# Expert layers' openings: one-hot tiles filled eight at a time, constants cast and row numbers multiplied in by GpSimd, and the second layer's exponentials and splits reordered

## The reference

```python
# expert layer 1, as the reference has it
logits = xf @ Wr + br
thresh = lax.top_k(logits, 2)[0][:, 1:2]
weights = softmax(where(logits >= thresh, logits, -inf))
h = gelu(einsum('td,edh->eth', xf, W1) + b1[:, None, :], approximate=False)
expert_out = einsum('eth,ehd->etd', h, W2) + b2[:, None, :]
out = einsum('etd,te->td', expert_out, weights)
```

## Time and profile before

| | |
|---|---|
| median of 3 runs | 2554.02 us (2550.81 to 2555.0) |
| the profiled execution's own time | 2552.48 us |
| its span in the trace | 2550.7 us |
| mean granted TensorE clock | 0.969 of full speed |
| PE busy | 2288.7 us, 90% of the span |
| PEld busy | 1394.3 us, 55% |
| DVE busy | 1919.7 us, 75% |
| ACT busy | 1900.7 us, 75% |
| POOL busy | 1809.4 us, 71% |
| DMA moved | 104.49 MB, mean 41 GB/s |
| opening of layer 0 in the trace | 1437 to 1483 us |
| opening of layer 1 in the trace | 2208 to 2259 us |

### The profile page before, as it was taken

One profiled execution on the slowest core, in us unless ns is written; L12 is line 12 of the kernel. 1 busy time (PEld: TensorE's weight loads), 2 busy tenths in 40 slices (PEclk: granted clock), 3 DMA queues, 4 the chain that ended last, 5 costly groups with the idle time before them and its releaser, 6 DMA issues. The chain is left out here.

```text
span 2550.7 us, 48415 instructions
## 1 busy us (share of the span) xinstructions
PE 2288.7 (90%) x16979; PEld 1394.3 (55%) x16980; DVE 1919.7 (75%) x3499; ACT 1900.7 (75%) x2979; POOL 1809.4 (71%) x1580
## 2 busy tenths in 40 slices
PE   5999999999999999999998589978988888689998
PEld 3454545444544545455544368845555555467777
DVE  7888778887778887777786556558899899676443
ACT  4787887878877878778787546638888889767555
POOL 2687877787777878787778567617787789646554
PEclk9999999999999999999999789989999999779999
DMA  5000000000000000000000365441112010375221
GB/s 151 1 1 1 27 1 1 1 1 1 27 1 1 1 1 1 1 1 1 1 1 1 107 154 144 115 102 45 46 34 50 22 43 11 105 187 140 44 42 24
DMA packets 90655, 104.49 MB, mean 41 GB/s; under 512 B 20626, under 2 KB 79971, under 8 KB 90419
## 3 DMA queue, kind: packets, MB, share of 16 engines
q1 hardware_dynamic: 68180, 78.21, 10.2%
q0 software_dynamic: 21696, 23.16, 5.7%
q10 hardware_dynamic: 544, 0.00, 0.0%
HBM read 66.65 MB, written 23.52 MB: 35 GB/s over the span
## 5 line engine op out<-in xcount | busy, mean ns | idle before, releaser
L432 POOL TENSOR_TENSOR a_acc<-a_acc,a_pf 128x512 f32<-128x512 f32 (+1 forms) x480 | 680.1, 1417 | 280.2 <-ACT a_pf L601 258.5
L906 DVE TENSOR_TENSOR a_pl<-a_pf,a_ph 128x512 f16<-128x512 f32 x448 | 470.3, 1059 | 25.1 <-ACT a_ph L607 25.1
L2221 POOL TENSOR_TENSOR c_pl<-c_pf,c_ph 128x512 f16<-128x512 f32 x320 | 377.2, 1210 | 117.1 <-ACT c_ph L2318 116.7
L601 ACT ACTIVATE a_pf<-a_psS 128x1024 f32<-128x1024 f32 (+1 forms) x288 | 281.1, 976 | 110.0 <-PE a_psS L624 102.5
L882 DVE TENSOR_REDUCE a_mx<-a_psA 128x1 f32<-128x512 f32 x504 | 330.4, 680 | 26.8 <-PE a_psA L681 25.5
L607 ACT ACTIVATE a_ph<-a_psS 128x1024 f16<-128x1024 f32 (+1 forms) x288 | 281.1, 976 | 0.0
L553 ACT ACTIVATE a_psS<-a_mb 128x1024 f32<-128x1024 f32 x255 | 248.6, 975 | 5.0
L1317 DVE TENSOR_TENSOR f_xn<-f_xn 128x256 f16<-128x256 f32 x312 | 130.0, 423 | 152.0 <-ACT f_xn L1286 106.8
L2554 DVE TENSOR_REDUCE c_wf<-c_psA 128x1 f32<-128x512 f32 x384 | 239.4, 677 | 6.2 <-PE c_psA L2390 5.3
L2311 ACT ACTIVATE c_pf<-c_psS 128x1024 f32<-128x1024 f32 x192 | 201.2, 1048 | 49.6 <-PE c_psS L2419 45.1
L776 PE MATMUL a_psO<-a_pl,a_vh 128*128 128x512 f16 (+1 forms) x544 | 206.9, 380 | 8.1 <-POOL a_pl L450 7.9
(11 more groups left out here) (366 smaller groups left out, 6311.4 us busy)
## 6 DMA issues: line engine op xcount, KB each, us to landing
f_stage<-in_L_ffn_w SPq DMA_DIRECT2D x16, 1024.0 KB
f_stage<-in_L_ffn_W SPq DMA_DIRECT2D x16, 1024.0 KB
c_kst<-c_khs SPq DMA_DIRECT2D x64, 100.1 KB, 2.2
a_cx<-in_ctx SPq DMA_DIRECT2D x4, 1536.0 KB
c_cx<-in_ctx SPq DMA_DIRECT2D x12, 512.0 KB, 4.0
f_xrow<-f_xn SPq DMA_DIRECT2D x8, 512.0 KB, 4.6
c_kst<-c_kls SPq DMA_DIRECT2D x32, 100.1 KB, 2.2
X<-in_x SPq DMA_DIRECT2D x4, 512.0 KB, 10.3
```

Of the source, the lines that this page charges most:

```text
L432: g.tensor_tensor(acc[0:k, p, :], acc[0:k, p, :], pf[0:k, q % RF, i, :], ALU.add).then_inc(s_acc, 1)
L601: act.activation(pf[0:r, q % RF, 0:k, :], psS[q % 2][0:r, 0:k, :], ACT.Exp, scale=SCALE).then_inc(s_pF, 1)
L906: v.tensor_tensor(pl[0:r, q % RP, i, :], pf[0:r, q % RF, i, :], ph[0:r, q % RP, i, :], ALU.subtract).then_inc(s_pL, 1)
L2221: g.tensor_tensor(pl[0:r, q % RP, i, :], pf[0:r, q % RF, i, :], ph[0:r, q % RP, i, :], ALU.subtract).then_inc(s_pG, 1)
```

## The change

It touches only `experts`.

- `lo` (f32) becomes `lo16` (f16) and `tid` becomes f16. The casts of `ilo`, `ihi`, `tid`, `dmp` (and `cf` in layer 1) move from DVE to GpSimd, behind its second `rstd`; GpSimd then counts s_pool up, and DVE waits for that before it fills `ohi`. In layer 1 DVE's copy of `b1` moves behind the chunk table.
- `olo` is filled by 4 instructions of eight tiles (128 x 1024) in place of 32 of one tile, and holds plain ones. The row number goes into `ohi` instead, by two multiplications on GpSimd (new semaphore s_hm), and TensorE waits for s_hm in place of s_hi.
- Layer 1: ACT's exponentials come ahead of all its splits of expert 0. DVE's split_low of expert 0 pieces 0 to 3 moves behind the lists (all eight stand there), and split_low of expert 1 pieces 0 to 3 moves behind chunk 0's turn (all eight stand there). TensorE's bias step NB2 moves behind the index products.
- The ties branch, which is taken only when a flag is above zero, reuses s_fin for s_tied.

```diff
@@ gpsimd, behind its second rstd
+            k[0] += 1
+            for to, of in ((ilo, iloi), (ihi, ihii), (tid, tidi), (dmp, dmpi)):
+                const(g.tensor_copy(to[:, :], of[:, :]))
+            if layer:
+                const(g.tensor_copy(cf[:, :], ci[:, :]))
+            g.wait_ge(s_const, k[0])
+            g.sem_inc(s_pool, 1)
@@ gpsimd, ahead of gather(0)
+            for q in range(2):
+
+                g.wait_ge(s_hi, q + 1)
+                g.tensor_tensor(ohi[:, q, :, :], ohi[:, q, :, :], tid[:, :].unsqueeze(2).broadcast_to([P, NT, HI]),
+                                ALU.mult).then_inc(s_hm, 1)
@@ scalar
             normalize(1)
-            for q in range(PH):
-                split_high(act, 0, q)
             if layer:
                 exponentials()
-            for q in range(PH, PIECES):
+            for q in range(PIECES):
                 split_high(act, 0, q)
@@ tensor
-                if layer and i == 2 * NT - 2 * NT // NLO:
-                    pe_weighted_bias(NB2)
-                pe.wait_ge(s_hi, q + 1)
+                pe.wait_ge(s_hm, q + 1)
...
-                for i in range(NB2 + 1, NT // 2):
+                for i in range(NB2, NT // 2):
                     pe_weighted_bias(i)
@@ vector
-            for to, of in ((ilo, iloi), (ihi, ihii), (tid, tidi), (dmp, dmpi)):
-                ch.step(v.tensor_copy(to[:, :], of[:, :]))
-            if layer:
-                v.wait_ge(s_b1, 1)
-                ch.step(v.tensor_copy(b1[:, :, :].rearrange("p e f -> p (e f)"), psY[1][:, 0:E * FT]))
-                ch.step(v.tensor_copy(cf[:, :], ci[:, :]))
...
-            if layer:
-                for q in range(PH):
-                    split_low(v, 0, q)
             v.wait_ge(s_rk, 1)
...
+            v.wait_ge(s_pool, 3)
             v.wait_ge(s_xst, 16 * (NQ + layer))
...
             for q in range(2):
-                for t in range(NT):
-                    ins = v.tensor_scalar(olo[:, q, t, :], ilo[:, :], lo[:, q, t:t + 1], tid[:, t:t + 1], ALU.is_equal, ALU.mult)
-                    if t % (2 * NT // NLO) == 2 * NT // NLO - 1:
-                        ins.then_inc(s_lo, 1)
+                for t in range(0, NT, 2 * NT // NLO):
+                    w = 2 * NT // NLO
+                    v.tensor_tensor(olo[:, q, t:t + w, :], ilo[:, :].unsqueeze(1).broadcast_to([P, w, P]),
+                                    lo16[:, q, t:t + w].unsqueeze(2).broadcast_to([P, w, P]), ALU.is_equal).then_inc(s_lo, 1)
...
-            for q in range(PH if layer else 0, PIECES):
+            for q in range(PIECES):
                 split_low(v, 0, q)
...
                 v.sem_inc(s_tab, 1)
-                for q in range(PH):
-                    split_low(v, 1, q)
+                v.wait_ge(s_b1, 1)
+                op(v.tensor_copy(b1[:, :, :].rearrange("p e f -> p (e f)"), psY[1][:, 0:E * FT]))
...
-                for q in range(PH, PIECES):
+                for q in range(PIECES):
                     split_low(v, 1, q)
```

More of the change, by code:

```diff
@@ L1078, in experts @@
         pos, posi = sb("pos", [P, 2, NT]), sb("posi", [P, 2, NT], I32)
-        lo, hi16 = sb("lo", [P, 2, NT]), sb("hi16", [P, 2, NT], F16)
+        lo16, hi16 = sb("lo16", [P, 2, NT], F16), sb("hi16", [P, 2, NT], F16)
         iloi, ihii, tidi, dmpi = sb("iloi", [P, P], I32), sb("ihii", [P, HI], I32), sb("tidi", [P, NT], I32), sb("dmpi", [P, IT], I32)
-        ilo, ihi, tid, dmp = sb("ilo", [P, P], F16), sb("ihi", [P, HI], F16), sb("tid", [P, NT]), sb("dmp", [P, IT])
+        ilo, ihi, tid, dmp = sb("ilo", [P, P], F16), sb("ihi", [P, HI], F16), sb("tid", [P, NT], F16), sb("dmp", [P, IT])
         void = sb("void", [P, NC, IT])
@@ L1121, in experts @@
         s_lo = sem("lo")
+        s_hm = sem("hm")
         s_id = sem("id")
@@ L1139, in experts @@
             s_fin = sem("fin")
-            s_tied = sem("tied")
         class Loop:
@@ L1396, in _ @@
                     sp.wait_ge(ties.yF, NTIE + 2)
-                    sp.dma_start(out.rearrange("b (t p) c -> p (b t) c", p=P), X[:, :, :]).then_inc(s_tied, 16)
-                    sp.wait_ge(s_tied, 16)
+                    sp.dma_start(out.rearrange("b (t p) c -> p (b t) c", p=P), X[:, :, :]).then_inc(s_fin, 16)
+                    sp.wait_ge(s_fin, 32)
         @block.gpsimd
@@ L1834, in _ @@
             op(v.tensor_scalar(posi[:, :, :], posi[:, :, :], P - 1, None, ALU.bitwise_and))
-            op(v.tensor_copy(lo[:, :, :], posi[:, :, :]))
-            op(v.tensor_tensor(hi16[:, :, :], pos[:, :, :], lo[:, :, :], ALU.subtract))
+            op(v.tensor_copy(lo16[:, :, :], posi[:, :, :]))
+            op(v.tensor_tensor(hi16[:, :, :], pos[:, :, :], lo16[:, :, :], ALU.subtract))
+            v.wait_ge(s_pool, 3)
             v.wait_ge(s_xst, 16 * (NQ + layer))
```

## The result

The change takes 2556.09 us (median of 14 runs, 2552.15 to 2562.13) against 2553.44 us for the kernel before (14 runs, 2546.89 to 2557.86). The ratio of the runs taken side by side is 1.0016, 95% interval 1.0009 to 1.0024: 4.1 us slower (0.0016 x 2553.44), between 2.3 and 6.1 us; the best value is less than the 0.2% called no difference above. The two medians by themselves are 2.7 us apart; I go by the ratio. The profiled execution took 2552.15 us (span 2550.4 us) and is the quickest of the 14, so totals of the two traces say little. I compare distances inside an opening. For layer 0 the count runs from DVE's `ohi` fills to `gidx`; for layer 1 from DVE's `rstdw` row.

The account below looks back on a forecast made before the run. DVE was taken to bound both openings up to the lists, with ACT's queue, the weights' path and chunk 2's rows behind layer 1's. Layer 0 -0.8 plus layer 1 +3.0 gave +2.2 us: 2556.2 against 2554.02, range 2549.5 to 2560.5.

Parts of the forecast that it names:

- Layer 0: Layer 0's opening up to the lists: fills save 2.6 us, contention costs 1.8 us, together -0.8 us.
- contention: GpSimd's multiplications beside DVE's fills: DVE loses 0.6 of the shared time, 1.8 us in layer 0.
- the casts: Layer 0: moving DVE's four casts (0.4 us) to GpSimd gains nothing, since DVE waits for the router's products anyway.
- rival D: New fills run at double rate: 2.1 us less in layer 0, nothing in layer 1, 2554.1 us; chance 0.05.
- E: The fills gain nothing: contention eats all 2.6 us of layer 0, 2557.0 us; chance 0.10.
- Layer 1, lists: Layer 1's opening: gidx comes 4.0 us earlier, with PE and DVE arriving together.
- The new wait of ACT: Layer 1: ACT waits 9.4 us for half 0 of expert 1, with bias copies 4 to 7 queued behind.
- Half 0 of expert 2: Layer 1, chunk 0: this weight load, requested later at 2262.6, lands 6 us after its request.
- rival B: Half 0 of expert 2 takes 9.3 us, PE restarts at its lower clock: +6.0 us, 2560 us; chance 0.22.
- the fifth piece: Layer 1, chunk 0: ACT's fifth piece of expert 2 comes 6.1 us after the first, +4.3 us against before.
- Given back: Layer 1, chunk 1: PE no longer waits for chunk 2's rows, which returns 1.3 us.
- Rival C: The gather chain sets the end, so layer 1's 4.0 us survive: -4.8 us or -6.6, put at 2548.5 us; chance 0.13.

Follow-up runs that it names:

- x4: The change with the two multiplications by the row number on DVE, between its ohi and olo fills, instead of GpSimd: 2558.14 us, ratio 1.0018.
- x2: The change with only the low splits of expert 1 pieces 0 to 3 back ahead of chunk 0's turn: 2553.44 us, ratio 1.0002.
- x5: The change without layer 1's four adding DMAs (add_base), so its output lacks the bias part: 2549.22 us, ratio 0.9977.
- x1: The change with layer 1's low splits of pieces 0 to 3 of experts 0 and 1 back in their old places: 2550.89 us, ratio 0.9992.
- x6: x1 with the two multiplications by the row number on DVE instead of GpSimd: 2549.49 us, ratio 0.9984.
- y3: x1 with layer 1's adding DMAs issued behind chunk 2's gather, once half 1 of expert 2 is in: 2552.36 us, ratio 0.9992.
- y4: The kernel before with layer 1's adding DMAs issued behind chunk 2's gather, once half 1 of expert 2 is in: 2558.13 us, ratio 1.0014.
- z3: x6 with layer 1's adding DMAs behind chunk 2's gather, without a wait for the weights: 2540.32 us, ratio 1.0016.
- z1: x1 with five small iotas on GpSimd (0.6 us) ahead of layer 1's adding DMAs: 2531.64 us, ratio 0.9988.
- x3: x1 with ACT's order and the place of bias step NB2 as in the kernel before: 2553.34 us, ratio 0.9996.
- z2: x3 with the two multiplications by the row number on DVE instead of GpSimd: 2535.60 us, ratio 1.0001.

## Why the prediction was right, and where its steps were not

The median came out 0.1 us from the forecast of 2556.2, and in the range. The kernel before measured 0.6 us lower in the larger set of runs, so the effect is +4.1 us by the ratio, not +2.2. That the median came so close is luck: the level lay 0.6 us lower than assumed and the difference of the medians (2.65 us) 0.4 us higher than forecast, and the two cancel. Step by step:

- **Layer 0, right.** Forecast -0.8, measured -1.0 (9.85 to 8.81). Fills undisturbed 4.62 us (forecast 4.5), contention 1.70 us (forecast 1.8), the casts worth nothing: `rstdw` to `ohi` is 11.85 us in both. Of the time in which a multiplication and an `olo` fill ran together (2.97 us in layer 0, 3.71 in layer 1) DVE lost 0.57 and 0.66, forecast 0.6. Rivals D and E fall: no fill ran at twice the rate (in x4 one takes 1.155 us for 128x1024), and not all of the gain was eaten. The tier table of the Trainium skill (VectorE: DVE Perf Modes), by which rival D halved the fills, isn't contradicted by that: the same page (What auto-detection actually checks) gives the doubled rate of such an operation only where every tensor is 16-bit with step ±1, and one operand of these fills is held over the inner dimension. The prediction left this condition out.
- **Layer 1, lists, right in kind.** Forecast -4.0, measured -4.65 in the change and -3.5 in x2 and x5. The difference is PE's clock in the four bias steps: a granted 0.73 of full speed on average in the profiled execution of the change, 0.50 in x2, after like idle stretches. The steps take 4.98 us at the one and 7.19 at the other. Windows of the change, then of x2 (PE, PEld, DVE, ACT, POOL busy, PEclk, DMA share, GB/s):

```profile
2229.40:2234.50 5.10, 5.02 (x19) 3.67 (x20) 5.10 (x3) 1.82 (x5) 4.16 (x2) 0.73 0.00 0
```

```profile
2230.70:2238.00 7.30, 7.23 (x19) 5.26 (x20) 7.21 (x5) 1.81 (x5) 3.86 (x2) 0.50 0.00 0
```

- **The new wait of ACT, right.** Forecast 9.4 us, measured 11.24. The request went out 24.17 us behind `rstdw` (forecast 24.7) and landed after 4.9 us (forecast 5.0). ACT came to the wait 2.4 us sooner than forecast, because of that clock; in x2, at 0.50, the wait is 10.36. That the 4.0 us of the lists would be spent by chunk 0's turn held: forecast +0.4 us, measured -0.2, and the first hidden block +0.1 (forecast +0.8).
- **Half 0 of expert 2, mis-sized: this is the step that failed.** "I take 6": it took 11.1 us, nearly twice. Its request was on time (39.94 us behind `rstdw`, forecast 40.5). I argued that it would be quicker than half 1 for its longer rows, and x5 shows how little those count: without adding DMAs half 0's packets (256 of 4 KB) pass in 3.3 us, half 1's (1024 of 1 KB) in 3.0. Half 0 lands there in 5.0 us, and what makes the rest is `add_base`: in the change its first packet goes 5.4 us behind the request (1.0 in x5), while packets of the second and third adding DMA go, and the 256 then take 5.0 us beside the fourth's. I also wrote that `add_base` starts as early as before; it starts 2.75 us earlier (34.80 against 37.55 behind `rstdw`), so the issue of the fourth adding DMA was about to end (5.36 us behind the first's start) at the request (5.14). The condition of rival B (over 8.4 us) was met.
- **So the fifth piece came later**: +7.9 us (2274.18 against 2271.17, each less its `rstdw`), forecast +4.3; rival B had +6.8. PE restarted at the lower clock level, as rival B had it (a granted 0.50 of full speed from 2269.0 to 2272.5), but the fifth piece came 5.9 us behind the first, no later than the 6.1 of the forecast.
- **Given back, right and a little more.** PE's 1.25 us for chunk 2's rows are gone, as forecast. From +7.9 at the fifth piece to +5.9 at chunk 2's turn and +4.6 at the end is more than that. It isn't the clock: from the turn of chunk 2 to that of chunk 5 the change takes 35.6 us and the kernel before 37.8, at a granted clock of 1.00 in both, and 0.9 us of this are lost again by the end. What shortens these chunks isn't known.
- **Rival C falls.** `gidx` was 4.65 us earlier and the end 4.6 us later; x1, x5 and x6 are faster than the change with fewer or shorter waits on `f_stage`, not with earlier lists (x1 has `gidx` 2.4 us later than the change).

The sum: -1.04 + 4.55 = +3.5 against a forecast of -0.8 + 3.0 = +2.2. The mechanism of layer 1 was the one named (the low splits are what frees the staging halves), the size of its second wait that of rival B. The forecast number was met more closely than its terms were.

## What to carry to other kernels

Before a step is moved off the path, ask what it frees: a split that reads a staging buffer is also the permission for the next load, and 2.4 us of work moved behind the lists held back a megabyte that takes 5 to 11 us. When a transfer must be priced, look at what else the queues carry at the time of the new request; rows with the nearest traffic (9.3 us beside adding DMAs) are worth more than rows with the nearest shape. And when a bulk transfer of low urgency is moved, its cost goes with it: y3, y4 and z3 each found some 7 us (6.8 to 7.8) at a load requested behind it.

## What the runs showed of the hardware

**Half 1 of expert 2 landed in one of two times beside the adding DMAs, and 0.3 us of order decided.** This half (1 MB), requested 1.74, 2.17 and 2.28 us behind the issue of the first of four adding DMAs (z1, before, x6), landed after 9.3, 9.3 and 9.2 us; requested 2.58, 2.65 and 2.74 us behind it (x3, x1, z2), after 13.7, 14.0 and 13.9, and 4.92 us behind it (x2) after 14.0. Nothing lies between, in one trace each. (Other halves took other times: 11.1 us in the change, 12.5 and 13.5 in y3 and y4.) z1, whose edit is aimed at this distance alone, speaks for the order.

The DMA packets in the traces show what differs. Each adding DMA is 512 packets of 1 KB, the half 1024. In z1, before and x6 the half's first packet goes 5.1 to 5.2 us behind the first adding DMA's issue, while that DMA's packets still pass (to 5.6 or 5.7); then the second one's first packet stands back until 8.3 to 8.6, and the half passes in 5.3 to 5.8 us. In x3, x1 and z2 the second adding DMA's packets follow the first's at once (at 5.4 to 5.6), the half's begin only at 6.0 to 6.2, and both streams pass side by side: the half takes 9.5 to 10.0 us. Windows of x6, then of x1, with the half in transfer (columns as above):

```profile
2256.50:2260.00 3.50, 3.50 (x35) 3.19 (x33) 2.67 (x6) 2.68 (x6) 2.59 (x3) 1.00 0.97 274
```

```profile
2261.00:2269.00 8.00, 4.13 (x38) 3.35 (x36) 1.84 (x4) 1.33 (x3) 3.20 (x4) 0.94 1.14 224
```

So in these six traces the half either came in ahead of the second adding DMA, or beside it. Why 0.3 us at the request become 0.8 to 1.1 us at the first packet stays open; the fourth adding DMA's issue starts 2.43 to 2.45 us behind the first's, just between the two groups, which may be chance. Edits that look unrelated (a few tenths on GpSimd or DVE) can so move a wait by 5 us; how much of that reaches the time of the kernel isn't clear of the noise (x1 0.9992, z1 0.9988).

**GpSimd beside DVE.** Two multiplications of 512 elements take 3.40 us beside DVE's fills: 1.42 us for the first, which ran partly beside an `ohi` fill, and 2.02 for the second, wholly beside `olo` fills, where L443 takes 1.03 to 1.05 us in its shortest and median row. DVE's first two fills take 2.06 us each there and 1.22 in x4. So both engines slow down while both work: DVE loses 1.70 of 2.97 shared us in layer 0 and 2.44 of 3.71 in layer 1, GpSimd about half of its second multiplication's time.
